# Attention kernel on one core: per-row means and deviations sent to DRAM one body earlier and fetched without a wait between

## The reference

```python
def _layer_norm(x, gamma, beta):
    mu = jnp.mean(x, axis=-1, keepdims=True)
    var = jnp.mean(jnp.square(x - mu), axis=-1, keepdims=True)
    return (x - mu) * jax.lax.rsqrt(var + LN_EPS) * gamma + beta
...
a = _layer_norm(audio_kv, ln_gamma, ln_beta)          # 8 x 512 x 1024
Q = (hidden_states @ Wq.T)                            # 8 x 512 x 1024, 16 heads of 64
K = (a @ Wk.T)
V = (a @ Wv.T)
scores = jnp.einsum('bhtd,bhsd->bhts', Q, K) * scale
scores = jnp.where(mask, scores, -inf)
attn = jax.nn.softmax(scores, axis=-1)
out = jnp.einsum('bhts,bhsd->bhtd', attn, V)
return hidden_states + jnp.tanh(gate) * (out @ Wo.T)
```

## Time and profile before

| | |
|---|---|
| median of 3 runs | 2043.04 us (2041.65 to 2044.86) |
| profiled execution, its own time | 2042.95 us |
| its span | 2041.2 us |
| PE busy | 1956.4 us, 96% |
| POOL busy | 1570.1 us, 77% |
| DVE busy | 1617.1 us, 79% |
| mean granted clock of PE | 0.982 of full speed |

### The profile page before, as it was taken

The page is one execution under the profiler, slowest core; times in us unless marked ns, Lnnn a source line. Parts: engine busy times, 40 slices in busy tenths (PEclk is TensorE's granted clock), DMA queues, the critical chain, the costliest instruction groups (busy, mean ns, idle before and its releaser), DMA issues.

```text
span 2041.2 us, 26143 instructions
## 1 busy us (share of the span) xinstructions
PE 1956.4 (96%) x8528; PEld 1583.0 (78%) x8528; DVE 1617.1 (79%) x2089; ACT 1287.7 (63%) x2375; POOL 1570.1 (77%) x851
## 2 busy tenths in 40 slices
PE   7899999999998999989999999998999989999998
PEld 5787778778887788877888778887788877888886
DVE  7688778778887688877888777887778867878878
ACT  5776866558655486555865558665586546856654
POOL 3999987589875898758976689766897668976664
PEclk9999999999999999999999999999999989999999
DMA  7566546544455444554456543564534745335432
GB/s 261 208 236 236 190 166 221 180 155 176 149 202 186 142 166 155 210 184 150 146 181 215 174 151 132 182 235 146 166 132 167 255 125 192 126 132 201 144 108 105
DMA packets 150039, 356.67 MB, mean 175 GB/s; under 512 B 63504, under 2 KB 67600, under 8 KB 149008
## 3 DMA queue, kind: packets, MB, share of 16 engines
q1 hardware_dynamic: 149904, 354.99, 50.6%
HBM read 303.54 MB, written 51.39 MB: 174 GB/s over the span
## 4 chain that ended last, share of the span: by engine, by line
PE 55%; POOL 12%; DMA 12%; DVE 11%; ACT 4%; SPq 3%; issue 3%; POOLq 0%; DVEq 0%; ACTq 0%
PE pj L487 10%; PE pj L489 10%; PE pj L491 10%; DMA rows<-rstd 5%; PE pv L434 4%; PE sc L440 4%; PE sc L444 4%; PE sc L441 4%; POOL a_lo L1207 3%; PE pv L435 3%; POOL p_lo L1165 3%; PE sc L414 3%; PE sc L415 3%; DVE mq L860 3%; DMA w_raw<-rows 2%
## 5 line engine op out<-in xcount | busy, mean ns | idle before, releaser
L1165 POOL TENSOR_TENSOR p_lo<-prob,p_hi 128x1024 fp32r<-128x1024 f32 x256 | 612.0, 2405 | 121.5 <-ACT p_hi L664 121.5
L487 PE MATMUL pj<-a_hi,w_hi 128*128 128x512 f32 x1024 | 401.7, 392 | 5.3 <-DVE qt L910 3.6
L491 PE MATMUL pj<-a_hi,w_lo 128*128 128x512 f32 x1024 | 400.0, 391 | 0.0
L489 PE MATMUL pj<-a_lo,w_hi 128*128 128x512 f32 x1024 | 399.4, 390 | 0.0
L860 DVE TRANSPOSE_TENSOR_REDUCE mq<-sc 128x32 f32<-128x1024 f32 x256 | 303.9, 1224 | 79.2 <-PE sc L415 78.3
L659 ACT ACTIVATE prob<-prob 128x1024 f32<-128x1024 f32 x256 | 271.4, 1060 | 92.1 <-DVE prob L882 91.5
L927 DVE SCALAR_TENSOR_TENSOR xy<-sc,tg_b,xy 128x1024 f32<-128x1024 f32 x244 | 305.4, 1273 | 15.6 <-PE sc L444 9.3
L882 DVE TENSOR_TENSOR prob<-sc,m_b 128x1024 f32<-128x1024 f32 x256 | 301.6, 1220 | 4.4
L1169 POOL TENSOR_TENSOR prob<-prob 128x1024 f32<-128x1024 f32 x126 | 302.1, 2398 | 0.0
L664 ACT CAST p_hi<-prob 128x1024 fp32r<-128x1024 f32 x256 | 269.3, 1052 | 3.8
L487 PE MATMUL pj<-x_hi,w_hi 128*128 128x512 f32 x512 | 214.4, 419 | 59.3 <-DMA w_lo<-kept_lo 47.4
(11 more groups left out here) (129 smaller groups left out, 3830.5 us busy)
## 6 DMA issues: line engine op xcount, KB each, us to landing
w_hi<-kept_hi SPq DMA_DIRECT2D x224, 512.0 KB, 4.0
w_lo<-kept_lo SPq DMA_DIRECT2D x224, 512.0 KB, 5.2
xy<-in_xT SPq DMA_DIRECT2D x32, 512.0 KB, 6.5
cx<-in_ctx SPq DMA_DIRECT2D x32, 512.0 KB, 5.6
kept_hi<-w_hi SPq DMA_DIRECT2D x32, 512.0 KB, 5.4
kept_lo<-w_lo SPq DMA_DIRECT2D x32, 512.0 KB, 6.1
out_y<-xy SPq DMA_DIRECT2D x7, 2048.0 KB, 9.8
cx<-in_ctxT SPq DMA_DIRECT2D x24, 512.0 KB, 5.4
```

Source lines behind the costliest of these rows:

```text
L487: pe.matmul(dst, w_hi[:, w, cols], s_hi[:, i], start=i == 0, stop=False)
L489: pe.matmul(dst, w_hi[:, w, cols], s_lo[:, i], start=False, stop=False)
L491: mm = pe.matmul(dst, w_lo[:, w, cols], s_hi[:, i], start=False, stop=i == KT - 1)
L1165: pool.tensor_tensor(p_lo[:, 2 * i:2 * i + 2], prob[:, h, 2 * i:2 * i + 2], f32(p_hi[:, 2 * i:2 * i + 2]), ALU.subtract).then_inc(pl_done, 1)
```

## The change

`spread_rows` is cut in two. `rows_out` holds its waits for the values and the four DMAs to `rows`, and stands at the end of SP's list for body 2 (pair 0) and body 3 (pair 1). `rows_in` holds the wait for these DMAs and the two fetches, and stands where `spread_rows` stood, behind `exchange_sums` of body 3 and body 4. No other engine's program changes. Lines behind the edit move down by three, and those from `batch` on by three to five.

```diff
-SPREAD_ROWS = {3: 0, 4: 1}
+ROWS_OUT, ROWS_IN = {2: 0, 3: 1}, {3: 0, 4: 1}
...
-            def spread_rows(b, pair):
+            def rows_out(b, pair):
                 sp.wait_ge(rstd_done, b * 2 + 3 + pair)
                 sp.wait_ge(z_done, b * TB + TB)
                 n = 2 * (b - 1) + pair
...
                 for s in (2 * pair, 2 * pair + 1):
                     for c, one in enumerate((nmean, rstd)):
                         sp.dma_start(rows[c, s].rearrange("(p o) -> p o", o=1), one[:, s:s + 1]).then_inc(row_out, 16)
+
+            def rows_in(b, pair):
+                n = 2 * (b - 1) + pair
                 sp.wait_ge(row_out, n * 64 + 64)
                 for c, one in enumerate((mean_row, rstd_row)):
                     sp.dma_start(one[:, pair * 2 * P:(pair + 1) * 2 * P],
...
                     exchange_sums(k - 1)
-                    if j in SPREAD_ROWS:
-                        spread_rows(b, SPREAD_ROWS[j])
+                    if j in ROWS_IN:
+                        rows_in(b, ROWS_IN[j])
                     if j == 0:
                         next_mask(b)
...
                     if j == 1:
                         store_y(b - 1, k)
+                    if j in ROWS_OUT:
+                        rows_out(b, ROWS_OUT[j])
```

## The result

| | before | changed |
|---|---|---|
| median | 2042.35 us (4 runs) | 1968.44 us (4 runs, 1967.38 to 1974.06) |
| profiled execution | 2042.95 us | 1974.06 us |
| span | 2041.2 us | 1972.3 us |
| mean granted clock of PE | 0.982 | 0.996 |

The ratio is 0.9643, 95% interval 0.9621 to 0.9665: 3.6% faster. The forecast was 1965.3 us, 3.8%. The execution that was profiled is the slowest of the four, 5.6 us above their median; it shows more of what was left than a typical one.

The account below looks back on a forecast made before the run. PE's pace was taken to bound the kernel, busy 1956.4 of 2041.2 us. Profiled 2042.95 less the 77.87 us excess gives 1965.1; with 0.2 for rests the forecast was 1965.3 us, range 1962.5 to 1981.

Parts of the forecast that it names:

- The size of the event: Bodies 4 and 5 of the six batches with preparation exceed PE's pace by 77.87 us, all of it to be won.
- What the profile was to show: Bodies 4 and 5 of batches 1 to 6 at 59.4 to 60 us, clock 1.00; waits for `row_out` and Q weights gone.
- one event seen from three engines: Twelve waits each of POOL (116.9 us), DVE (75.3) and PE (47.4) share one cause, SP's wait for the `rows` writes.
- Pair 0 and pair 1: Fetch at 637.6 in body 3, 667.3 in body 4; POOL waits about 1 us for pair 0, none for pair 1.
- rival 2: POOL becomes the next bound in bodies 4 and 5, giving 12 to 36 us back, 1977 to 2001; chance 0.06.
- The landing among loads: Writes to `rows` issued among weight loads land in 9 to 12 us, at most 18.9, hidden by 15.4 us available.
- they cost the list nothing: Four DMAs added behind body 2's output weights take 2.4 us of issue, done at 622.6 before V weights due at 623.07.
- Rival 1: Writes ahead of the V weights and sums' exchange delay the sums, 1970 to 2015; chance 0.10 with writes visible in part.
- a 512-byte write: SP's wait of 9 us in `spread_rows` is for this write's acknowledgement, not bandwidth; 9.06 taken over the skill's 2 us.

Follow-up runs that it names:

- out_behind_v: The changed kernel with the four DMAs to `rows` issued behind the V weights at the head of body 3's and 4's list: 1966.14 us, ratio 0.9674.
- turned_whole: The kernel before, send, wait and fetch together, with DVE transposing means and deviations so the DMAs write 16 runs of 128 bytes: 1965.86 us, ratio 0.9668.
- q_first: The kernel before with `spread_rows` whole, but behind the Q weights' loads in SP's list: 2091.22 us, ratio 1.0294.
- held_clean: turned_split with SP held behind the fetch of the rows in bodies 3 and 4 until DVE's fourth subtraction: 1988.84 us, ratio 0.978.
- turned_split: The changed kernel with DVE transposing means and deviations in 32 x 32 blocks before they are sent: 1965.73 us, ratio 0.9666.
- after_again: The changed kernel, unaltered, run again on another chip: 1968.22 us, ratio 0.9686.
- twice: The changed kernel with each DMA to `rows` issued a second time to another part of DRAM, the wait counting all eight: 1979.54 us, ratio 0.9738.
- one_run: The changed kernel with each DMA to `rows` sending 512 constant bytes in one run, context means and deviations left out: 1965.66 us, ratio 0.9666.
- one_run_before: The kernel before with each DMA to `rows` sending 512 constant bytes in one run, context means and deviations left out: 1965.93 us, ratio 0.9674.

## Why the prediction was right, and where it was off

- **The size of the event.** Counting the excess of bodies 4 and 5 over PE's pace (77.87 us), not a sum of waits, was right: 71.2 of it went in the profiled execution, and all of it in `out_behind_v` and `turned_whole`, whose bodies 3 to 5 are within 0.05 us of 29.7. The 77.87 us hold for the chip on which they were read; on the others the change wins 64 us. What the profile was to show came in three of six batches; in the other three the clock or the length was off, as above.
- **One cause.** The wait was the cause, but I let "one event seen from three engines" stand for one path. There are two behind it: POOL's late start (`q_first`: PE loses with all weights in time) and the list held back (`held_clean`: 23 us by itself). How the 64 us divide between them in the first kernel is not shown. The split opens both, so the sum did not depend on it. A change that opened only one would have been forecast wrong by my step.
- **Pair 0 and pair 1.** Two errors nearly cancelled here, which is luck. The first fetch was forecast 14.6 us into the body; it left at 14.5 to 16.7, since the sums ahead of it were late. And the rows landed sooner: issue to landing 3.5 us at the median against 5.4, and for the second fetch of a pair, where 5.2 was taken, 3.1 to 5.1. POOL waited five times, for pair 0 alone, 2.6 us at most; about 1 us, six times, was forecast. POOL kept up, and rival 2 did not come.
- **The landing among loads.** 4.7 to 11.9 us over all DMAs to `rows`, with a median of 8.3. The forecast was for the last of each four, 9 to 12 us with 18.9 as a bound; these took 7.7 to 11.9, ten of twelve inside 9 to 12. SP never waited for it.
- **The step that was mis-sized: "they cost the list nothing".** I looked only at what is queued behind the four DMAs, the V weights, which are due 20 us later. They did land late, `w_hi` in 7.9 to 11.8 us and `w_lo` in 11.0 to 13.4, where `turned_split` has 3.4 to 4.5 and 4.3 to 6.6, and no engine waited for them. But the `w_lo` of the output weights, issued just ahead of the writes, also landed late, and it is due 10.9 us after its issue; it took 11.4 to 13.1 us at four of the twelve places. It cost 8.3 us in the profiled execution and 1.5 in that of `after_again`; `twice` makes it 11 us more, and in `one_run`, `out_behind_v` and `turned_split` PE does not wait. Their medians are 2.1 to 2.6 us below `after_again`, so it is probably most of the 3 us between forecast and median; differences that small the times do not show.
- **Rival 1** (the sums held) came, and small: behind the writes and the V weights the sums took more than 1.4 us at ten of the twelve places, up to 3.6, within the slack of some 7; in `turned_split` they did at two. In `twice` they did at all twelve, up to 4.0. The prediction had this as a sign of being wrong, and it was there, at no cost. The Trainium skill's rule that a semaphore's increment lands only after every earlier write of its DMA engine (DMA: Bandwidth & Descriptors, "Queues, rings and completion order") would make the V weights complete after the writes. At ten of the twelve places of the changed kernel's trace the V weights' `w_hi` does land after the last write; at two it lands first by the issue and landing times of the profile, as above: 402.08 + 8.9 = 411.0 against 400.69 + 11.9 = 412.6. And that rule says nothing of a load issued ahead, which is where the cost was.
- **The price behind it all** I took as given: 9.06 us for the acknowledgement of "a 512-byte write". `one_run_before` shows that it is not the price of a small write but of one of 128 elements of 4 bytes from 128 partitions: 512 bytes in one run keep SP 0.9 us at most. The 2 us that the prediction takes from the Trainium skill (DMA: Bandwidth & Descriptors, "Anatomy of one DMA") are given there for DMAs that GpSimd issues; these are issued by SP.

What stays open is how the short writes hold back a load that was issued ahead of them, and why it is 5 us at one place and 13 at another. The runs show that they do, not by what. Nor do they show whether it is the writes to DRAM or the reads from 128 partitions that take the time.

## What to carry to other kernels

When a DMA that moves little takes long to land, look at its number of separate elements before moving its wait: a transpose of 0.2 us on DVE and 16 runs of 128 bytes did here what the reordering of the queue did, and left no late load behind. When a DMA is put at a new place in a queue, check the loads ahead of it for their due time as well as those behind it. And where one wait delays two paths, try each alone: each may keep a part of the loss, and neither part need be the whole.

## What the runs showed of the hardware

Four DMAs of 128 elements of 4 bytes from SBUF to DRAM took 5.6 to 9.6 us to land with nothing else in flight, at a DMA share of 0.02, where the same 512 bytes in one run, or in 128-byte runs, kept SP waiting 0.9 us at most. Twice as many of them did not make the V weights behind them land noticeably later (`w_hi` 10.0 to 11.9 us against 7.9 to 11.8). Loads of 512 KB beside them landed in up to 13.4 us when issued behind them and up to 13.1 when issued ahead, where `turned_split` has at most 6.6 at the same places.
